# First layer of a two-layer transformer kernel: turned banks put together, queries and keys projected at a round's end

## The reference

```python
q = jnp.einsum('qdh,bcd->bhcq', Q, x) * sq
k = jnp.einsum('qdh,bcd->bhcq', K, x) * sq
v = jnp.einsum('vdh,bcd->bhcv', V, x) * sv
att = jnp.einsum('bhcq,bhCq->bhcC', q, k) / d_query
att = jnp.where(causal, att, -jnp.inf)
p = jax.nn.softmax(att, axis=-1)
y = jnp.einsum('bhcC,bhCv->bhcv', p, v)
z = jnp.einsum('dvh,bhcv->bcd', W, y) * (math.sqrt(d_embed / d_value) / num_heads)
```

## Time and profile before

| what | value |
|---|---|
| median of 3 runs | 1193.75 us (1191.75 to 1194.74) |
| the profiled execution's own time | 1194.1 us |
| its span | 1192.2 us |
| TensorE busy | 1171.3 us, 98% |
| VectorE busy | 983.1 us, 82% |
| ScalarE busy | 810.1 us, 68% |
| GpSimd busy | 407.2 us, 34% |
| mean granted TensorE clock | 0.997 |

### The profile page before, as it was taken

One profiled execution on the slowest core, in us unless ns is written; L12 is line 12 of the kernel. 1 busy time (PEld: TensorE's weight loads), 2 busy tenths in 40 slices (PEclk: granted clock), 3 DMA queues, 4 the chain that ended last, 5 costly groups with the idle time before them and its releaser, 6 DMA issues.

```text
span 1192.2 us, 23821 instructions
## 1 busy us (share of the span) xinstructions
PE 1171.3 (98%) x8908; PEld 897.7 (75%) x8908; DVE 983.1 (82%) x1918; ACT 810.1 (68%) x2182; POOL 407.2 (34%) x364
## 2 busy tenths in 40 slices
PE   8999999999999999999999999999999999999998
PEld 6777687767777777677767776777777777767866
DVE  5988588979897989698969886989797878988886
ACT  6885577557755775677567756775577668767775
POOL 1317420640064007300630073006400768526820
PEclk9999999999999999999999999999999999999999
DMA  7004200310041003100410041004100410000000
GB/s 261 2 30 147 88 1 30 125 62 2 30 125 63 1 30 130 58 1 30 134 54 2 30 137 51 2 30 140 47 2 30 151 37 2 10 10 19 1 11 28
DMA packets 44292, 63.93 MB, mean 54 GB/s; under 512 B 8144, under 2 KB 18384, under 8 KB 43920
## 3 DMA queue, kind: packets, MB, share of 16 engines
q1 hardware_dynamic: 44176, 62.39, 16.2%
HBM read 59.48 MB, written 2.88 MB: 52 GB/s over the span
## 4 chain that ended last, share of the span: by engine, by line
PE 82%; DVE 9%; ACT 5%; issue 2%; DMA 1%; SPq 1%; POOL 0%; ACTq 0%; DVEq 0%; POOLq 0%
PE psum L1507 13%; PE psum L1529 12%; PE psum L1454 12%; PE psum L65 10%; PE psum L67 9%; PE psum L66 9%; PE psum L1564 4%; DVE mneg L1146 3%; ACT probs L766 3%; PE psum L1464 2%; PE psum L1756 1%; PE psum L1533 1%; PE psum L1819 1%; PE psum L1406 1%; DVE sg L1196 1%
## 5 line engine op out<-in xcount | busy, mean ns | idle before, releaser
L766 ACT ACTIVATE probs<-psum,mneg 128x256 f32<-128x256 f32 (+3 forms) x528 | 253.0, 495 | 166.5 <-DVE mneg L1146 165.5
L1146 DVE TENSOR_REDUCE mneg<-psum 128x2 f32<-128x1024 f32 (+2 forms) x320 | 245.2, 819 | 46.5 <-PE psum L1464 44.1
L1137 DVE COPY pt<-psum 128x512 f32<-128x512 f32 x320 | 205.7, 682 | 47.4 <-PE psum L1507 45.5
L1507 PE MATMUL psum<-ident,probs 128*128 128x128 f32 x1600 | 210.7, 276 | 3.8 <-DVE pt L1137 1.6
L1507 PEld LDWEIGHTS psum<-ident,probs 128*128 128x128 f32 x1600 | 178.2, 141 | 31.8 <-ACT probs L766 12.2
L573 POOL TENSOR_TENSOR qk_lo<-sg,qk_hi 128x512 fp32r<-128x512 f32 x64 | 92.4, 1450 | 159.0 <-ACT qk_hi L820 159.0
L1529 PE MATMUL psum<-pt,v_all 128*64 128x384 f32 (+5 forms) x1088 | 142.6, 412 | 0.0
L537 POOL TENSOR_TENSOR rstd<-var,mhalf 128x4 f32<-128x4 f32 x7 | 7.1, 1010 | 383.4 <-DVE var L1032 383.4
L1454 PE MATMUL psum<-qk_hi 64*128 64x512 f32 (+7 forms) x640 | 114.2, 353 | 5.4 <-DVE qk_lo L1131 3.6
L1529 PEld LDWEIGHTS psum<-pt,v_all 128*64 128x64 f32 (+1 forms) x1088 | 69.7, 135 | 63.0 <-issue 50.6
L65 PE MATMUL psum<-xt_hi,gu_hi 128*128 128x512 f32 x272 | 111.1, 409 | 0.7 <-DVE sg L1186 0.6
(11 more groups left out here) (276 smaller groups left out, 2506.0 us busy)
## 6 DMA issues: line engine op xcount, KB each, us to landing
crow<-weights SPq DMA_DIRECT2D x256, 128.0 KB, 2.9
rrow<-sums SPq DMA_DIRECT2D x128, 128.0 KB, 3.0
gu_raw<-in_gu SPq DMA_DIRECT2D x1, 2176.0 KB, 11.4
x_all<-in_x SPq DMA_DIRECT2D x8, 256.0 KB, 5.5
out_rows<-x_all SPq DMA_DIRECT2D x7, 256.0 KB, 2.3
down_raw<-in_down SPq DMA_DIRECT2D x1, 1088.0 KB, 13.5
wqkv_raw<-in_wqkv SPq DMA_DIRECT2D x1, 896.0 KB, 6.7
wqkv_raw<-in_wqkv SPq DMA_DIRECT2D x1, 512.0 KB, 4.8
```

Of the source, the lines that this page charges most:

```text
L766: last = act.activation(probs[:, h * HALF + PROB[t]:h * HALF + PROB[t] + w], bank[score_bank(rnd, c) + h][:, o:o + w], ACT.Exp, bias=mneg[ ...
L1137: dve.tensor_copy(turned_rows(rnd)[:, s % 2, :, 3 - s // 2, :], turn_bank(rnd, s).rearrange("p (j q) -> p j q", q=P)).then_inc(pt_ready, 1)
L1146: last = dve.tensor_reduce(mneg_h[:, :, t], psum[:, b:b + 2, o:o + P * (t + 1)], AX, ALU.max, negate=True)
L1507: last = nc.tensor.transpose(turn_bank(rnd, s)[:, i * P:(i + 1) * P], probs[:, v:v + P], ident[:, :])
```

## The change

In the rounds `p` of 0 to 5 of each batch, all five turns stand together, and the projection of pair `n + 2` follows them at the round's end. ScalarE takes the fifth turned bank ahead of the two roundings, and VectorE copies all four of its turned banks ahead of the rests. In `score_group`, chunk 2 of `n` stands ahead of chunk 0 of `n + 1` (in rounds 0 to 6; round 7 has no next one). In round 0 chunk 2 now waits for the rests of pair 1, because their keys lie in bank 5. In round 6 the turns stay in two parts, and VectorE only copies turn 3 ahead of the inversion. Nothing is added or removed in arithmetic.

```diff
--- before.py
+++ after.py
@@ -853,14 +853,14 @@
                     if p < PAIRS - 1:
                         next_exps(n + 1, 0)
                         next_exps(n + 1, 1)
-                    if p < PAIRS - 2:
-                        round_q(n + 2, SCALE0)
-                        round_k(n + 2)
                     if p == PAIRS - 2:
                         copy_combt(b)
                     if p == PAIRS - 1:
                         load_table(ACT.Silu)
                     take_tile1(n)
+                    if p < PAIRS - 2:
+                        round_q(n + 2, SCALE0)
+                        round_k(n + 2)
                     if b == 0 and p >= PAIRS - len(DOWN_PIECES):
 
                         u = DOWN_PIECES[p - PAIRS + len(DOWN_PIECES)]
@@ -1212,13 +1212,11 @@
                     if p < PAIRS - 1:
                         row_maxima(n + 1, 0)
                     route(b, p)
-                    take_turned(n, range(3))
+                    take_turned(n, range(TURNS - 1 if p < PAIRS - 1 else 3))
                     invert_sums(n)
                     if p < PAIRS - 2:
                         rest_q(n + 2, SCALE0)
                         rest_k(n + 2)
-                    if p < PAIRS - 1:
-                        take_turned(n, [3])
                     if p == PAIRS - 2 and b:
                         add_rows(b - 1)
                 n = b * PAIRS + PAIRS - 1
@@ -1622,14 +1620,16 @@
                     pe.wait_ge(pt_ready, (n - 1) * (TURNS - 1) + 3)
                 score_masks(n, 1, True)
                 score_products(n, 1, n % 2, ROWS0, True).then_inc(scored, 1)
+                if p:
+                    pe.wait_ge(pt_ready, n * (TURNS - 1))
+                    pe.wait_ge(pt4_ready, n)
+                else:
+                    pe.wait_ge(qk_lo_ready, (n + 1) * 2 + 2)
+                score_products(n, 2, n % 2, ROWS0)
                 if p < PAIRS - 1:
                     pe.wait_ge(qk_lo_ready, (n + 1) * 2 + 2)
                     pe.wait_ge(exp_done, exp_count(n, 0))
                     score_products(n + 1, 0, (n + 1) % 2, ROWS0)
-                if p:
-                    pe.wait_ge(pt_ready, n * (TURNS - 1))
-                    pe.wait_ge(pt4_ready, n)
-                score_products(n, 2, n % 2, ROWS0)
                 score_masks(n, 2).then_inc(scored, 1)
                 if p < PAIRS - 1:
                     score_masks(n + 1, 0).then_inc(scored, 1)
@@ -1652,7 +1652,7 @@
                         pe.wait_ge(x1_ready, b)
                     turn_step0(n, 0)
                     return
-                for s in range(3):
+                for s in range(TURNS if p < PAIRS - 2 else 3):
                     turn_step0(n, s)
                 if p < PAIRS - 2:
                     if p:
@@ -1668,8 +1668,8 @@
                     if b:
                         pe.wait_ge(pt_ready, n * (TURNS - 1) + 1)
                         turn_acc(b - 1)
-                turn_step0(n, 3)
-                turn_step0(n, 4)
+                    turn_step0(n, 3)
+                    turn_step0(n, 4)
 
             def first_head(b):
```

## The result

The changed kernel takes 1200.68 us (median of 4 runs, 1200.18 to 1203.5), the kernel before, run beside it, 1194.24 us. The ratio is 1.0059 with a 95% interval of 1.0045 to 1.0074, so 5.4 to 8.8 us slower. The forecast was 1200.5. The profiled execution took 1200.95 us.

The account below looks back on a forecast made before the run. TensorE's list of products was taken to bound the rounds. Seams 0, wait 6.7 us and 0 for the rest sum to 6.7 us; on the median of 1193.75 this gives 1200.5 us, range 1193.5 to 1206.5.

Parts of the forecast that it names:

- What bounds: In a round TensorE is busy for all of 8.35 us; order can only cheapen its list or bring in a wait.
- Part 1, seams: Turns 3 and 4 ahead of the projection: the 0.10 us seam before the masks stays, gain 0.
- Part 2, the chain: Keys' projection, ScalarE rounding, VectorE rests, TensorE's 512-wide chunk: it comes 0.11 us late, making rounds 0.14 us longer.
- S: Start of the last of the six projecting passes on TensorE, from which times in a round are counted.
- 0.14 us per round: Growth of a round with a projection: 0.11 us from the chain's lateness and some 0.04 from the restart.
- The restart: TensorE's six 512-wide products after a wait take 0.80 us instead of 0.76, some 0.04 us per round.
- the sum: Whole kernel: 0 for seams, 6.7 us for the wait, 0 for the rest, giving 6.7 us more.
- 48 times: The wait happens wherever a projection stands in a round, rounds 0 to 5 of 8 batches: 6.7 us.
- Part 3: ScalarE's and VectorE's moved instructions fit where nobody waits and cost nothing; ScalarE has 0.1 us to spare.
- Part 4: Single edits: round 0's chunk 2 waited for rests before too, round 6's inversion is not waited for; each 0.
- what would show it: Changed profile: rounds 1 to 5 about 8.50 us, TensorE idle about 0.1 us before 512-wide products some 48 times.

Follow-up runs that it names:

- the rounded part ahead of the wait: Changed kernel with the 512-wide chunk's first pass waiting only for the rounded keys, the wait for the rests behind it: 1193.34 us, ratio 0.9997.
- turns together alone: Changed kernel with the score chunks in the old order, the 512-wide chunk ahead of the 256-wide one: 1219.33 us, ratio 1.0218.
- the chunk order alone: Kernel before with only the 256-wide chunk put ahead of the 512-wide one (the hunk of `score_group`): 1207.47 us, ratio 1.0116.

## Why the prediction was right

**What bounds.** Right for rounds 1 to 5: TensorE's list fills them, and the change could only make the list cheaper or bring in a wait. In a first round TensorE did wait, 0.14 us for ScalarE's copy, and the change took that away; the prediction did not see it.

**Part 1, seams.** Right in the choice of 0. Projection to masks took 0.33 us (416.13 to 416.46), as in the single row of batch 0, so the tenth of a microsecond does not belong to the turns; it is there behind the projection as well. With the wait taken out (the rounded part ahead of it) the merged turns and the exchanged chunks together were worth 0.01 us per round. The Trainium skill, page TensorEngine Tiling (Array Packing), section Key Properties, has a rule that fits, the drain at a change of tiling mode (all 128 rows to 64 here); the trace agrees, with 0.10 us for the step, but no run here varied the mode alone.

**Part 2, the chain.** Right in mechanism and nearly in size. Forecast and measured: rounding of the keys S + 0.43 and S + 0.43, rest from S + 1.06 and S + 1.07, wide chunk S + 1.79 and S + 1.81, last masks S + 2.59 and S + 2.62. The changed kernel and two of the runs show the same S + 1.81 under three orders on TensorE.

**Mis-sized: 0.14 us per round.** Measured were 0.19. Of the 0.05, 0.03 are in the chain and what follows it: the handover to VectorE took 0.04 instead of 0.03 us and its instruction 0.69 instead of 0.68, and the six wide products 0.81 instead of 0.80. Some 0.03 are in turns and projection: 3.40 us to S, where the parts of before add up to 3.37. The restart was taken as 0.04 us, because the wide chunk's 0.76 of before were the yardstick; those hold 0.05 of their own, from following 128-wide products. Against its real 0.71 the restart costs 0.10. The 0.05 of the following did no harm to the sum, since they come back as the narrow chunk's (0.41 instead of 0.36).

**Wrong: 48 times.** The chain's lateness is there behind all 48 projections, but in the 8 first rounds the moved projection also loses its wait for ScalarE's copy, so they hardly change. The trace has 7.4 us in the 40 other rounds and 0.2 in the first ones, where the sum had 6.7.

**The total is better than its terms.** 1200.5 against 1200.68 looks closer than the working was. The 0.05 us were missing in 40 rounds (2 us too little), and 8 rounds were counted that cost next to nothing (1 us too much). What is left, 1 us too little, is hidden by the scatter of the medians: the kernel before had 1193.75 at the forecast, 1194.24 beside the change, and 1193.4 and 1193.2 in the two larger sets of the experiments. That it came out to 0.2 us is luck; that it came out to a few us is not.

**Part 3.** Right: ScalarE's and VectorE's new places cost nothing. The fifth bank's copy ends at 415.77 and the queries' rounding starts at 415.87, so the margin of 0.1 us was as forecast. Undoing ScalarE's order costs 12 us.

**Part 4.** Right: the 8 waits of first rounds for the rests (3.6 us) stayed, and round 6 takes 6.84 us to its successor in both kernels.

**Wrong: what would show it.** I expected TensorE idle in front of the wide chunk some 48 times. The profile has no such idle time. The gaps are inside the tails of the records before them, and a reader who had gone by the list of waits would have found no cause.

## What to carry to other kernels

Where one engine's list fills the time, look for the chains that leave it and come back, and write down how early each comes back; here it was 0.34 us, and any work that stands between the two ends is cover, whatever else it is good for. When the cover must go, the wait can often be moved inside the consumer, behind the part that needs only the first half of the producer's work. And two edits that each lose can need each other: judge them together before undoing one.

## What the runs showed of the hardware that was not expected

A wait of only 0.09 us on TensorE, at a granted clock of 1.00, costs another 0.10 us behind it: in the changed kernel the first pair of 512-wide products takes 0.34 us until the next (417.94 to 418.28), and where the same pair follows the same products without a wait it takes 0.24 (the rounded part ahead of the wait, 415.62 to 415.86). A wait of 0.5 us costs no more (0.34, turns together alone). And gaps of this size do not show as idle time of TensorE; they show only in start-to-start distances, and in the mean of the group that waits (353 to 367 ns over 640 products). Gaps of 0.14 us (the projection of a first round in the kernel before) and of 0.22 us (the chunk order alone, all but one) are missing from the list of waits too.
